# Embedding features: ScalarE multiplies x by the frequencies, VectorE takes off the rounding constant and subtracts the product in one operation

## The chip, the cores and the metric

The kernel runs on one core of one Trainium2 chip. A time is the device time of one execution in microseconds (us). The kernel before was timed three times: 1026.73, 1033.01 and 1031.65 us, so its median is 1031.65 us. The engines are TensorE (PE in the profile, its weight loads PEld), VectorE (DVE), ScalarE (ACT), GpSimd (POOL) and SyncE (SP, which only issues DMAs here).

## What is computed

A vision tower with one layer. The change lies in the first stage, the embedding of the tokens:

```
def _L0_tok_ref(xyz, freq_bands, W):          # xyz (4, 3, 512, 192), 6 frequencies 1, 2, 4 ... 32
    xb = 2.0 * jnp.pi * xyz[..., None] * freq_bands
    feat = jnp.concatenate([jnp.sin(xb), jnp.cos(xb)], axis=-1)
    feat = feat.reshape(b, n, -1)
    return jnp.einsum('bnf,of->bno', feat, W)  # 6912 features to 192
...
h = _L0_tok_ref(x, ...)
h = concatenate([cls_tok, h], axis=1)          # (4, 513, 192)
h = h + _L0_attn_ref(_layernorm(h), ...)       # attention with relative positions, 8 heads
h = h + _L0_ffn_ref(_layernorm(h), ...)        # attention over 12 heads, layer norms, 2 of 8 experts
```

The argument of the sine is first reduced to a part of one turn: with p = x*f, the kernel forms p minus the whole number nearest to p, and takes the sine of 2 pi times that. The cosine is the sine of pi/2 minus 2 pi times the absolute value of the same remainder. The nearest whole number comes from adding 12582912 (MAGIC) and taking it off again in float32.

## The kernel before

`embed_phase` works through four images. An image has 15 groups of features: groups 0 to 11 are "pairs" (two chunks of 128 input rows at one frequency, so a tile is 128 partitions x 1024), groups 12 to 14 are singles (128 x 512). A group passes through the engines like this:

- VectorE: `shift` (L202, near = x*f + MAGIC), `whole` (L207, near = near - MAGIC), `reduce` (L215, turn = x*f - near), `absolute` (L221, the absolute value of turn, put into near again).
- ScalarE: `group` takes the sine (L330, feat slot 0) and the cosine (L332, feat slot 1). For a pair, `first_parts` (L343) then rounds the features of the second chunk to a shorter format (parts 0), and VectorE's `rest` (L232) gives what is left (parts 1). In the first image each pair's weights are split the same way (L337 on ScalarE, L226 on VectorE).
- TensorE: 8 products with feat on plain float32 (16 MATMUL rows of L400), then for a pair 16 with the parts (L416 to L420). They add up in four PSUM banks over the whole image. When the last group is in, VectorE's `take_sums` copies the sums out (L238, L241) and takes statistics (L244, L249); TensorE may begin the next image's group 0 only when the first of the L241 additions is done.

Nothing plans the order: each engine has its program in written order, and semaphores join them. The tiles `feat`, `parts`, `near` and `turn` have three slots each (NF = 3), so group g uses slot g % 3. `feat_free` counts the groups that TensorE is done with; the sine of group g waits until group g - 3 is counted. `take_sums(b-1)` stands in VectorE's program at group 1 of image b, behind `rest` of group 0. `take_roots(b-1)` (two square roots on ScalarE, L348, which need another activation table) stands behind group 3, and `normalize(b-1)` (L253 to L261), which waits for it, at group 4 on VectorE. SP reloads x for the next image when `turn_done` says that the last group on a chunk has been reduced, and after the last x it fills a scratch area with zeros by 20 DMAs.

Of the kernel before, what the change touches and what calls it, by code (L numbers as in the profile page):

```python
# [8 lines left out]
ALU = mybir.AluOpType  # L9
ACT = mybir.ActivationFunctionType  # L10
# [7 lines left out]
B = 4  # L18
# [29 lines left out]
MAGIC = 12582912.0  # L48
NO_SIGN = 0x7FFFFFFF
TWO_PI = 6.283185307179586  # L50
EPS = 1e-5
BIG = 1e30
GROUPS = [(c0, 2, f) for c0 in (0, 2) for f in range(BANDS)] + [(4, 1, j) for j in range(BANDS // 2)]
UNITS = [(c0 + i, f) for c0, n, f in GROUPS for i in range(n)]
NE = len(GROUPS)
# [8 lines left out]
def stand_alone(eng, passed):  # L64


    eng.sem_inc(passed, 1)


def embed_phase(nc, s):  # L70

    NF = 3
    sem = s.sem
    x_in, w_in = [sem(f"x_in{c}") for c in range(5)], [sem(f"w_in{g}") for g in range(NE)]
    raw_in = [sem(f"raw_in{g}") for g in range(NE)]
    freq_in, ident_in, cls_in, zeroed = sem("freq_in"), sem("ident_in"), sem("cls_in"), sem("zeroed")
    consts_set, edges_set = sem("consts_set"), sem("edges_set")
    shifted, rounded, turn_done, aturn_done = sem("shifted"), sem("rounded"), sem("turn_done"), sem("aturn_done")
    sin_done, cos_done, feat_free, passed = sem("sin_done"), sem("cos_done"), sem("feat_free"), sem("turns_passed")
    w_hi, w_lo, hi_done, lo_done = sem("w_hi"), sem("w_lo"), sem("hi_done"), sem("feat_lo")  # L80
    pairs = [g for g in range(NE) if GROUPS[g][1] == 2]
# [9 lines left out]
    first_unit = [sum(n for _, n, _ in GROUPS[:g]) for g in range(NE)]  # L91
    with ExitStack() as ctx:
        sb = lambda n, sh, dt=F32: ctx.enter_context(nc.sbuf_tensor(n, sh, dt))
        x = sb("x", [128, 5, N])
        w = sb("w", [128, 2 * NE, D])
        raw = s.place.rearrange("p (g j n) -> p g j n", g=NPAIR, j=2)
        feat = sb("feat", [128, NF, 2, 2, N])
        w_parts = sb("w_parts", [128, NPAIR, 2, 2, D], F32R)
        parts = sb("parts", [128, NF, 2, 2, N], F32R)
        near = sb("near", [128, NF, 2, N])  # L100
        turn = sb("turn", [128, NF, 2, N])
        aturn = near
        tokens, h1_tok = sb("tokens", [128, 4, D]), sb("h1_tok", [128, 4, D])
        b2_rows, base = sb("b2_rows", [128, D]), sb("base", [128, 4, D])
        stats, mean_var = sb("stats", [128, 4, 6]), sb("mean_var", [128, 4, 2])
        roots, inv = sb("roots", [128, 2, 4]), sb("inv", [128, 2, 4])
        half_pi, eps = sb("half_pi", [128, 1]), sb("eps", [128, 2])
        freq = sb("freq", [128, NU])
# [78 lines left out]
        def _(dve):  # L187
# [4 lines left out]
            def shift(b, g, first):  # L192
                c0, n, f = GROUPS[g]
                u, r = first_unit[g], g % NF
                if f == 0:
                    for c in range(c0, c0 + n):
                        dve.wait_ge(x_in[c], b * 16 + 16)
                if g >= NF or not first:
                    dve.wait_ge(cos_done, b * NE + g - NF + 1)
                if not first:  # L200
                    stand_alone(dve, passed)
                dve.tensor_scalar(near[:, r, 0:n, :], x[:, c0:c0 + n, :], freq[:, u:u + 1], MAGIC, ALU.mult, ALU.add).then_inc(shifted, 1)  # L202

            def whole(b, g):
                n, r = GROUPS[g][1], g % NF
                dve.wait_ge(shifted, b * NE + g + 1)
                dve.tensor_scalar(near[:, r, 0:n, :], near[:, r, 0:n, :], MAGIC, None, ALU.subtract).then_inc(rounded, 1)  # L207

            def reduce(b, g, first):
                c0, n, f = GROUPS[g]  # L210
                u, r = first_unit[g], g % NF
                dve.wait_ge(rounded, b * NE + g + 1)
                if g >= NF or not first:
                    dve.wait_ge(sin_done, b * NE + g - NF + 1)
                dve.scalar_tensor_tensor(out=turn[:, r, 0:n, :], in0=x[:, c0:c0 + n, :], scalar=freq[:, u:u + 1], in1=near[:, r, 0:n, :],  # L215
                                         op0=ALU.mult, op1=ALU.subtract).then_inc(turn_done, 1)

            def absolute(b, g):
                n, r = GROUPS[g][1], g % NF
# [50 lines left out]
            def cls_norm():  # L270
                dve.wait_ge(cls_rooted, 1)
                dve.reciprocal(cls_inv[:, :], cls_roots[:, :]).then_inc(cls_rooted, 1)
                dve.wait_ge(cls_rooted, 2)
                for k, row in enumerate((s.y_cls[:, :], cls_row[:, 1, :])):
                    dve.tensor_scalar(row, cls_row[:, 0, :], cls_mean_var[:, 0:1], cls_inv[:, k:k + 1],
                                      ALU.subtract, ALU.mult).then_inc(cls_rows, 1)

            def image(b, first=False, more=True):
                for g in range(NE):
                    if first and g == 4:  # L280
                        cls_statistics()
                    if first and g == 8:
                        cls_norm()
                    if g + 1 < NE:
                        whole(b, g + 1)
                    elif more:
                        whole(b + 1, 0)
                    reduce(b, g, first)
                    if g + 2 < NE:
                        shift(b, g + 2, first)  # L290
                    elif more:
                        shift(b + 1, g + 2 - NE, False)
                    absolute(b, g)
                    if g - 1 in pairs:
                        rest(b, g - 1)
                    if first and g in pairs:
                        split_weights(g)
                    if not first and g == 1:
                        take_sums(b - 1)
                    if not first and g == 4:  # L300
                        normalize(b - 1)

            dve.wait_ge(freq_in, 16)
            shift(0, 0, True)
            shift(0, 1, True)
            whole(0, 0)
            image(0, first=True)
            dve.wait_ge(cls_flipped, 1)
            dve.tensor_copy(cls_col[:, :], cls_flip[0:DC, 0:2]).then_inc(cls_cols_set, 1)
# [5 lines left out]
            with dve.Fori(1, B - 1) as b:  # L315
                image(b)
# [5 lines left out]

        @block.scalar
        def _(act):
            def group(b, g, first):
                n, r = GROUPS[g][1], g % NF
                act.wait_ge(turn_done, b * NE + g + 1)
                if g >= NF or not first:
                    act.wait_ge(feat_free, b * NE + g - NF + 1)
                act.activation(feat[:, r, 0, 0:n, :], turn[:, r, 0:n, :], ACT.Sin, scale=TWO_PI).then_inc(sin_done, 1)  # L330
                act.wait_ge(aturn_done, b * NE + g + 1)
                act.activation(feat[:, r, 1, 0:n, :], aturn[:, r, 0:n, :], ACT.Sin,  # L332
                               bias=half_pi[:, :], scale=-TWO_PI).then_inc(cos_done, 1)

            def split_weights(g):
                act.wait_ge(raw_in[g], 16)
                act.copy(w_parts[:, g, :, 0, :], raw[:, g]).then_inc(w_hi, 1)  # L337

            def first_parts(b, g):
                r = g % NF  # L340
                act.wait_ge(sin_done, b * NE + g + 1)
                act.wait_ge(cos_done, b * NE + g + 1)
                act.copy(parts[:, r, 0], feat[:, r, :, 1, :]).then_inc(hi_done, 1)  # L343

            def take_roots(i):
                act.wait_ge(aggregated, i * 4 + 4)
                for k in range(2):
                    root = act.activation(roots[:, k, :], mean_var[:, :, 1], ACT.Sqrt, bias=eps[:, k:k + 1],  # L348
                                          scale=1.0 + EPS * k)
                root.then_inc(rooted, 1)  # L350

            def take_h1(i):
                for c in range(2):
                    act.wait_ge(h1_flipped, i * 2 + 2 + c + 1)
                    act.activation(s.h1T[0:DC, c, bass.ds(i, 1), 1:L].rearrange("p b n -> p (b n)"), flip[c][0:DC, :], ACT.Copy,
                                   scale=norm1[:, c:c + 1]).then_inc(h1_out, 1)

            act.wait_ge(consts_set, 3)
            act.sem_inc(rooted, 1)
            act.sem_inc(h1_out, 2)  # L360
            for g in range(NE):
                if g == 6:
                    act.wait_ge(cls_stated, 2)
                    for k in range(2):
                        root = act.activation(cls_roots[:, k:k + 1], cls_mean_var[:, 1:2], ACT.Sqrt, bias=eps[0:1, k:k + 1], scale=1.0 + EPS * k)
                    root.then_inc(cls_rooted, 1)
                group(0, g, True)
                if g in pairs:
                    split_weights(g)
                    first_parts(0, g)  # L370
            with act.Fori(1, B) as b:
                for g in range(NE):
                    group(b, g, False)
                    if g in pairs:
                        first_parts(b, g)
                    if g == 3:
                        take_roots(b - 1)
                    if g == 10:
                        take_h1(b - 1)
            take_roots(B - 1)  # L380
            take_h1(B - 1)

# [1964 lines left out]
```

## Time and profile before

| what | value |
|---|---|
| median of three runs | 1031.65 us |
| profiled execution, its own time | 1030.35 us |
| its span (what the profile covers) | 1028.6 us |
| granted TensorE clock, mean over the span | 0.949 of full speed |
| PE busy over the span | 911.2 us (89%) |
| PEld busy over the span | 798.0 us (78%) |
| DVE busy over the span | 721.2 us (70%) |
| ACT busy over the span | 653.4 us (64%) |
| the embedding, first DMA to last feature product | about 0 to 294 us |

The shares are averages over stages that differ. What the change does must be read in the first 300 us. A granted clock of 1.00 is 2.4 GHz and 0.50 is 1.2 GHz. In the first microseconds of the program the view says 1.00 although the matmuls there take about twice as long as later.

### The profile page before, as it was taken

The numbers are of one execution on the slowest core, as the hardware profiler recorded it, in microseconds if no ns is written. First come the engines' busy times: TensorE is split into PE (matmuls) and PEld (weight loads), VectorE is DVE, ScalarE is ACT, GpSimd is POOL, SyncE is SP. The second block draws the span as 40 slices with busy tenths as digits, with TensorE's granted clock in tenths as the row PEclk, the third lists the DMA queues.
The fourth block names the chain that finished last, engine by engine and source line by source line (L and its number), as shares of the span: only waits on it lengthen the run. The fifth ranks groups of instructions, "written<-read, shape, count | busy, mean of one in ns | idle before, by whom it ended". The sixth has DMA issues, their size and how long they took to land. (4 is left out here: it accounts for less than half of the span.)

```text
span 1028.6 us, 20033 instructions
## 1 busy us (share of the span) xinstructions
PE 911.2 (89%) x6459; PEld 798.0 (78%) x6459; DVE 721.2 (70%) x1690; ACT 653.4 (64%) x1223; POOL 141.9 (14%) x204
## 2 busy tenths in 40 slices
PE   5999999999987898889887988799699995799995
PEld 5899999999975777567666766677498874799993
DVE  7899979979833885478637864697566245688764
ACT  5766757848625886588748864797553332686661
POOL 1000000000000244114411431054300000000000
PEclk9999999999988999999999999999799997799995
DMA  8003100089703684269416951596300120533101
GB/s 264 22 21 96 37 31 25 31 129 154 119 17 109 191 278 128 66 188 295 136 52 184 290 157 35 166 299 186 104 1 1 32 77 16 163 108 108 55 1 62
DMA packets 83798, 114.06 MB, mean 111 GB/s; under 512 B 12271, under 2 KB 44476, under 8 KB 83724
## 3 DMA queue, kind: packets, MB, share of 16 engines
q1 hardware_dynamic: 83724, 113.18, 39.8%
q8 instruction: 34, 0.56, 0.2%
q14 instruction: 40, 0.33, 0.1%
HBM read 62.31 MB, written 47.67 MB: 107 GB/s over the span
## 5 line engine op out<-in xcount | busy, mean ns | idle before, releaser
L400 PE MATMUL psum<-w,feat 128*128 128x192 f32 x960 | 168.2, 330 | 13.7 <-ACT feat L330 10.2
L400 PEld LDWEIGHTS psum<-w,feat 128*128 128x128 f32 x960 | 156.9, 192 | 14.6 <-issue 10.1
L615 POOL TENSOR_SCALAR a_scores<-a_scores,a_inv 112x514 f32<-112x514 f32 (+1 forms) x160 | 112.9, 707 | 290.8 <-DVE a_inv L964 290.3
L949 DVE CUSTOM_DVE_ANT_0 a_scores<-psum,a_bias 112x514 f32<-112x514 f32 (+1 forms) x160 | 109.8, 688 | 49.2 <-PE psum L688 42.1
L837 ACT ACTIVATE a_scores<-a_scores,a_least 112x514 f32<-112x514 f32 (+1 forms) x160 | 116.6, 729 | 13.7 <-DVE a_least L949 13.1
L418 PE MATMUL psum<-w_parts,parts 128*128 128x384 f32 x368 | 113.5, 373 | 3.3 <-DVE parts L232 2.8
L701 PE MATMUL psum<-ident,a_scores 112*112 112x112 f32 (+1 forms) x800 | 102.3, 260 | 14.1 <-DVE a_probsT L959 8.2
L330 ACT ACTIVATE feat<-turn 128x1024 f32<-128x1024 f32 (+1 forms) x60 | 58.4, 974 | 85.7 <-DVE turn L215 53.9
L688 PE MATMUL psum<-a_kh,a_q 128*112 128x258 f32 (+1 forms) x320 | 101.2, 337 | 7.1 <-DVE a_q L919 4.2
L701 PEld LDWEIGHTS psum<-ident,a_scores 112*112 112x112 f32 (+1 forms) x800 | 77.5, 136 | 35.6 <-POOL a_scores L615 18.4
L642 PE MATMUL psum<-h1T,place 96*128 (+3 forms) x320 | 86.9, 410 | 13.3 <-DVEq L912 6.9
L420 PE MATMUL psum<-w_parts,parts 128*128 128x192 f32 x384 | 96.6, 252 | 0.0
L832 ACT COPY a_probsT<-psum 112x336 f32<-112x336 f32 (+1 forms) x160 | 66.6, 416 | 39.2 <-PE psum L701 35.2
L688 PE MATMUL psum<-a_kl,a_q 128*112 128x258 f32 (+1 forms) x320 | 85.6, 287 | 0.0
L671 PE MATMUL psum<-a_table,a_qpos 96*112 96x257 bf16 (+1 forms) x320 | 66.3, 289 | 16.2 <-ACT a_pos L824 14.2
L824 ACT COPY a_pos<-psum 112x514 f32<-112x514 f32 (+1 forms) x100 | 58.9, 589 | 33.4 <-PE psum L671 27.0
L642 PEld LDWEIGHTS psum<-h1T,place 96*128 96x128 f32 (+1 forms) x320 | 60.6, 204 | 24.0 <-DVEq L912 8.2
L418 PEld LDWEIGHTS psum<-w_parts,parts 128*128 128x128 f32 x368 | 69.2, 188 | 5.4 <-issue 5.3
L420 PEld LDWEIGHTS psum<-w_parts,parts 128*128 128x128 f32 x384 | 73.3, 191 | 0.0
L959 DVE COPY a_probsT<-psum 112x224 f32<-112x224 f32 (+1 forms) x160 | 58.8, 367 | 17.2 <-PE psum L701 16.8
L688 PEld LDWEIGHTS psum<-a_kh,a_q 128*112 128x112 f32 (+1 forms) x320 | 55.3, 173 | 19.8 <-issue 12.7
L215 DVE SCALAR_TENSOR_TENSOR turn<-x,freq,near 128x1024 f32<-128x1024 f32 (+1 forms) x60 | 70.2, 1170 | 0.0
(285 smaller groups left out, 1822.6 us busy)
## 6 DMA issues: line engine op xcount, KB each, us to landing
shear<-a_pos SPq DMA_DIRECT2D x128, 224.9 KB, 3.7
a_bias<-shear SPq DMA_DIRECT2D x128, 224.4 KB, 3.8
shear<-zero SPq DMA_DIRECT2D x20, 448.9 KB, 16.4
e_fc<-in_e_fc_dram SPq DMA_DIRECT2D x16, 384.0 KB, 3.9
x<-in_xT_dram SPq DMA_DIRECT2D x20, 256.0 KB, 3.0
e_proj<-in_e_proj_dram SPq DMA_DIRECT2D x8, 576.0 KB, 5.3
shear<-a_pos SPq DMA_DIRECT2D x32, 130.5 KB
a_bias<-shear SPq DMA_DIRECT2D x32, 130.3 KB
```

The lines of the kernel that those rows point to most:

```text
L215: dve.scalar_tensor_tensor(out=turn[:, r, 0:n, :], in0=x[:, c0:c0 + n, :], scalar=freq[:, u:u + 1], in1=near[:, r, 0:n, :], op0=ALU.mult, ...
L400: mm = pe.matmul(sums[m][:, 0:D], feat[:, r, j, 0, 128 * m:128 * m + 128], w[:, k, :], start=begins, stop=ends)
L418: pe.matmul(sums[m][:, 0:2 * D], f(0), w_parts[:, g, j, :, :].rearrange("p a n -> p (a n)"), start=False, stop=False)
L420: mm = pe.matmul(sums[m][:, 0:D], f(1), w_parts[:, g, j, 0, :], start=False, stop=False)
L615: pool.tensor_scalar(row, row, inv[0:TILES[g % NT][1], g % TT:g % TT + 1], 1.0, ALU.mult, ALU.mult).then_inc(weighed, 1)
L642: mm = pe.matmul(out[:, 0:HALF], wt[0:rows, c, 128 * p:128 * p + 128], x, start=c == 0, stop=c == 1)
L671: mm = pe.matmul(pairs[2][w][0:r, 0:HALF], qpos[:, h, i0:i0 + r], table[:, w * HALF:w * HALF + HALF], start=True, stop=True)
L688: mm = pe.matmul(pairs[score_pair(g)][w][0:r, 0:HALF + 1], q[:, h, i0:i0 + r], k[:, h, w * HALF:w * HALF + HALF + 1], start=k is kh, stop= ...
L701: mm = pe.transpose(pairs[3][jb // 3][0:TILE, TILE * (jb % 3):TILE * (jb % 3) + r], scores[0:r, g % TT, TILE * jb:TILE * jb + TILE], s.ide ...
L832: act.copy(probsT[:, slot(g // NT), 0:3, i0:i0 + r], src).then_inc(put_a, 1)
L837: act.activation(scores[0:r, g % TT, 0:PADL], scores[0:r, g % TT, 0:PADL], ACT.Exp, bias=least[0:r, g % TT:g % TT + 1], scale=-1.0, accum_ ...
L949: dve.tensor_tensor_reduce(halves(scores[0:r, g % TT, 0:PADL]), psum2(score_pair(g), r), halves(bias[0:r, g % MR, :]), -1.0 / 8, BIG, ALU. ...
```

## The change

VectorE's `whole` goes. ScalarE gets a new step, `scale_x`: it writes x*f into `scaled_x`, which is no tile of its own but slot r of `feat[:, :, 0]`, the place where the sine of the same group is written later. VectorE's `reduce` now reads near and `scaled_x` and gives (near - MAGIC) - x*f, the remainder with its sign turned, so the scale of the sine becomes -2 pi. On ScalarE the order is `scale_x` of group g + 1, then sine and cosine of group g (`waves`), and what followed. The wait for `feat_free` moves from the sine of group g to `scale_x` of group g, with the same count (group g - 3 done). VectorE's program is turned too: `reduce` of g, then `shift` of g + 1, where it had been `whole` of g + 1, `reduce` of g, `shift` of g + 2. The wait of `reduce` for an old sine goes, and one for `scaled` comes.

```
+        scaled_x = feat[:, :, 0]
...
-            def whole(b, g):
-                n, r = GROUPS[g][1], g % NF
-                dve.wait_ge(shifted, b * NE + g + 1)
-                dve.tensor_scalar(near[:, r, 0:n, :], near[:, r, 0:n, :], MAGIC, None, ALU.subtract).then_inc(rounded, 1)
-
-            def reduce(b, g, first):
-                c0, n, f = GROUPS[g]
-                u, r = first_unit[g], g % NF
-                dve.wait_ge(rounded, b * NE + g + 1)
-                if g >= NF or not first:
-                    dve.wait_ge(sin_done, b * NE + g - NF + 1)
-                dve.scalar_tensor_tensor(out=turn[:, r, 0:n, :], in0=x[:, c0:c0 + n, :], scalar=freq[:, u:u + 1], in1=near[:, r, 0:n, :],
-                                         op0=ALU.mult, op1=ALU.subtract).then_inc(turn_done, 1)
+            def reduce(b, g):
+                n, r = GROUPS[g][1], g % NF
+                dve.wait_ge(shifted, b * NE + g + 1)
+                dve.wait_ge(scaled, b * NE + g + 1)
+                dve.scalar_tensor_tensor(out=turn[:, r, 0:n, :], in0=near[:, r, 0:n, :], scalar=MAGIC, in1=scaled_x[:, r, 0:n, :],
+                                         op0=ALU.subtract, op1=ALU.subtract).then_inc(turn_done, 1)
...
+                    reduce(b, g)
                     if g + 1 < NE:
-                        whole(b, g + 1)
+                        shift(b, g + 1, first)
...
         @block.scalar
-            def group(b, g, first):
+            def scale_x(b, g, first):
+                c0, n, f = GROUPS[g]
+                u, r = first_unit[g], g % NF
+                if f == 0:
+                    for c in range(c0, c0 + n):
+                        act.wait_ge(x_in[c], b * 16 + 16)
+                if g >= NF or not first:
+                    act.wait_ge(feat_free, b * NE + g - NF + 1)
+                act.activation(scaled_x[:, r, 0:n, :], x[:, c0:c0 + n, :], ACT.Copy, scale=freq[:, u:u + 1]).then_inc(scaled, 1)
+
+            def waves(b, g):
                 n, r = GROUPS[g][1], g % NF
                 act.wait_ge(turn_done, b * NE + g + 1)
-                if g >= NF or not first:
-                    act.wait_ge(feat_free, b * NE + g - NF + 1)
-                act.activation(feat[:, r, 0, 0:n, :], turn[:, r, 0:n, :], ACT.Sin, scale=TWO_PI).then_inc(sin_done, 1)
+                act.activation(feat[:, r, 0, 0:n, :], turn[:, r, 0:n, :], ACT.Sin, scale=-TWO_PI).then_inc(sin_done, 1)
...
+            def image(b, more):
                 for g in range(NE):
-                    group(b, g, False)
+                    if g + 1 < NE:
+                        scale_x(b, g + 1, False)
+                    elif more:
+                        scale_x(b + 1, 0, False)
+                    waves(b, g)
                     if g in pairs:
                         first_parts(b, g)
                     if g == 3:
                         take_roots(b - 1)
```

How the change moves instructions is seen in the order of an engine's program; a bracket names the semaphores that a row waits for. On ScalarE, where images 0 and 1 meet: before, from the sine of the last group (128x512) to the features of group 0 of the next image (L330 sine, L332 cosine, L343 parts).

```order
L330 ACTIVATE feat<-turn 128x512 [waits feat_free,turn_done]
L332 ACTIVATE feat<-near,half_pi 128x512 [waits aturn_done]
L371 UNCONDITIONAL_BRANCH
L371 ISA
L329 REGISTER_ALU [waits turn_done]
L330 ACTIVATE feat<-turn 128x1024 [waits feat_free]
L332 ACTIVATE feat<-near,half_pi 128x1024 [waits aturn_done]
L343 CAST parts<-feat 128x1024 [waits cos_done,sin_done]
```

The same place with the change (L321 is `scale_x`, of group 0 in the first row and of group 1 in the sixth; L326 the sine, L328 the cosine, L338 the parts):

```order
L321 ACTIVATE feat<-x,freq 128x1024 [waits feat_free,x_in1,x_in0]
L326 ACTIVATE feat<-turn 128x512 [waits turn_done]
L328 ACTIVATE feat<-near,half_pi 128x512 [waits aturn_done]
L387 UNCONDITIONAL_BRANCH
L387 ISA
L321 ACTIVATE feat<-x,freq 128x1024 [waits feat_free]
L325 REGISTER_ALU
L326 ACTIVATE feat<-turn 128x1024 [waits turn_done]
L328 ACTIVATE feat<-near,half_pi 128x1024 [waits aturn_done]
L338 CAST parts<-feat 128x1024 [waits cos_done,sin_done]
```

The sine of group 0 stood behind a wait for TensorE's group 12 of the image before; now it stands behind `scale_x` of group 1, which waits for group 13.

On ScalarE, at the square roots behind group 3 of an image: before, from the roots to the parts of group 4.

```order
L348 ACT_TABLE_LOAD
L348 ACTIVATE roots<-mean_var,eps 128x4 [waits aggregated]
L348 ACTIVATE roots<-mean_var,eps 128x4
L327 REGISTER_ALU
L330 ACT_TABLE_LOAD [waits feat_free]
L330 ACTIVATE feat<-turn 128x1024 [waits turn_done]
L332 ACTIVATE feat<-near,half_pi 128x1024 [waits aturn_done]
L343 CAST parts<-feat 128x1024 [waits cos_done,sin_done]
```

With the change, from the parts of group 3 to the sine of group 4:

```order
L338 CAST parts<-feat 128x1024 [waits cos_done,sin_done]
L341 ISA
L343 ACT_TABLE_LOAD
L343 ACTIVATE roots<-mean_var,eps 128x4 [waits aggregated]
L343 ACTIVATE roots<-mean_var,eps 128x4
L321 ACTIVATE feat<-x,freq 128x1024 [waits feat_free]
L325 REGISTER_ALU
L326 ACT_TABLE_LOAD
L326 ACTIVATE feat<-turn 128x1024 [waits turn_done]
```

The roots and both table loads now have `scale_x` of group 5 among them, and that waits for TensorE's group 2 where the sine of group 4 had waited for group 1.

At the program's start ScalarE now has one table load more, and its first one waits for x (L321 `scale_x` of groups 0 and 1, L326 the sine of group 0):

```order
L321 ACT_TABLE_LOAD [waits consts_set,freq_in,x_in1]
L321 ACTIVATE feat<-x,freq 128x1024 [waits x_in0]
L321 ACTIVATE feat<-x,freq 128x1024
L326 ACT_TABLE_LOAD
L326 ACTIVATE feat<-turn 128x1024 [waits turn_done]
```

Before, one load stood there that waited for constants only; the sine followed it.

## Rows read from the trace of the kernel before

**Rows 1.** Windows: busy time of each engine in image 0 and image 1
```profile
core 0: us, PE busy (x) PEld busy (x) DVE busy (x) ACT busy (x) POOL busy (x), PEclk, DMA share, GB/s
24.31:78.59 54.28, 51.03 (x324) 48.87 (x323) 48.54 (x71) 37.60 (x44) 0.00 (x0) 1.00 0.06 21
88.24:156.18 67.94, 67.94 (x444) 67.64 (x444) 61.54 (x94) 45.34 (x47) 1.81 (x1) 1.00 0.08 26
```

**Rows 2.** Waits in 0 to 300 us: total, times, longest
```profile
PE psum L400 <- DVE tokens L241: 3.6, 3, 1.7
```

**Rows 3.** Lines by form: count, busy us, mean ns, idle before and its releasers
```profile
L215 DVE SCALAR_TENSOR_TENSOR turn<-x,freq,near 128x1024 f32<-128x1024 f32 x48 | 61.3, 1277 | 0.0
L232 DVE TENSOR_TENSOR parts<-feat,parts 128x1024 fp32r<-128x1024 f32 x48 | 58.4, 1217 | 0.6 <-ACT parts L343 0.6
L332 ACT ACTIVATE feat<-near,half_pi 128x1024 f32<-128x1024 f32 x48 | 55.0, 1146 | 6.3 <-DVE near L221 6.2
L330 ACT ACTIVATE feat<-turn 128x1024 f32<-128x1024 f32 x48 | 50.9, 1060 | 55.4 <-DVE turn L215 51.8 <-PE psum L400 2.6 <-PE psum L420 0.8
L343 ACT CAST parts<-feat 128x1024 fp32r<-128x1024 f32 x48 | 50.4, 1049 | 3.1
L202 DVE TENSOR_SCALAR near<-x,freq 128x1024 f32<-128x1024 f32 x48 | 35.8, 747 | 15.3 <-ACT feat L332 11.1 <-DMA x<-in_xT_dram 4.2
L207 DVE TENSOR_SCALAR near<-near 128x1024 f32<-128x1024 f32 x48 | 33.6, 702 | 0.2 <-DVE h1T L312 0.2
L221 DVE TENSOR_SCALAR near<-turn 128x1024 uint32<-128x1024 uint32 x48 | 32.8, 684 | 0.0
```

**Rows 4.** Timeline, DVE, where image 0 ends: start us, us, engine, line, op
```profile
85.65 1.22 DVE L232 TENSOR_TENSOR parts<-feat,parts 128x1024 fp32r<-128x1024 f32 x1
86.78 1.14 DVE L238 COPY tokens<-psum 128x192 f32<-128x192 f32 x4
87.85 1.14 DVE L241 TENSOR_TENSOR tokens<-tokens,psum 128x192 f32<-128x192 f32 x4
```

**Rows 5.** Timeline, PE, groups 0, 1 and 2 of image 1
```profile
88.24 2.87 PE L400 MATMUL psum<-w,feat 128*128 128x192 f32 x16 [1.67 <-DVE tokens L241]
93.42 2.78 PE L400 MATMUL psum<-w,feat 128*128 128x192 f32 x16
98.34 2.78 PE L400 MATMUL psum<-w,feat 128*128 128x192 f32 x16
```

**Rows 6.** Timeline, ACT, groups 2 to 4 of image 1 with the roots between
```profile
93.98 1.15 ACT L332 ACTIVATE feat<-near,half_pi 128x1024 f32<-128x1024 f32 x1 [0.20 <-DVE near L221]
95.22 1.05 ACT L343 CAST parts<-feat 128x1024 fp32r<-128x1024 f32 x1
...
100.48 1.28 ACT L348 ACT_TABLE_LOAD   x1
...
102.27 1.28 ACT L330 ACT_TABLE_LOAD   x1
103.57 1.06 ACT L330 ACTIVATE feat<-turn 128x1024 f32<-128x1024 f32 x1
104.53 1.14 ACT L332 ACTIVATE feat<-near,half_pi 128x1024 f32<-128x1024 f32 x1
```

**Rows 7.** Timeline, DVE, `normalize` at group 4 of image 1, first instruction and the one behind
```profile
103.39 0.19 DVE L253 RECIPROCAL inv<-roots 128x8 f32<-128x8 f32 x1
...
106.16 0.69 DVE L207 TENSOR_SCALAR near<-near 128x1024 f32<-128x1024 f32 x1
```

**Rows 8.** Timeline, the start: x arrives for DVE, first products on PE
```profile
5.10 1.42 DVE L202 TENSOR_SCALAR near<-x,freq 128x1024 f32<-128x1024 f32 x2 [4.16 <-DMA x<-in_xT_dram]
...
10.15 5.09 PE L400 MATMUL psum<-w,feat 128*128 128x192 f32 x16 [10.15 <-ACT feat L330]
```

**Rows 9.** Windows, PE alone, three stretches of a later stage: busy, PEclk, DMA
```profile
516.80:518.40 1.60, 0.00 (x0) 1.00 0.25 62
...
519.90:523.30 3.40, 3.40 (x17) 0.50 0.22 56
...
734.90:748.50 13.60, 8.69 (x37) 0.50 0.70 196
```

More of the change, by code:

```diff
@@ L77, in embed_phase @@
     consts_set, edges_set = sem("consts_set"), sem("edges_set")
-    shifted, rounded, turn_done, aturn_done = sem("shifted"), sem("rounded"), sem("turn_done"), sem("aturn_done")
+    scaled, shifted, turn_done, aturn_done = sem("scaled"), sem("shifted"), sem("turn_done"), sem("aturn_done")
     sin_done, cos_done, feat_free, passed = sem("sin_done"), sem("cos_done"), sem("feat_free"), sem("turns_passed")
@@ L283, in image @@
                         cls_norm()
+                    reduce(b, g)
                     if g + 1 < NE:
-                        whole(b, g + 1)
+                        shift(b, g + 1, first)
                     elif more:
[L287 to L292, printed above, removed]
+                        shift(b + 1, 0, False)
                     absolute(b, g)
@@ L304, in _ @@
             shift(0, 0, True)
-            shift(0, 1, True)
-            whole(0, 0)
             image(0, first=True)
@@ L324, in _ @@
         def _(act):
-            def group(b, g, first):
+            def scale_x(b, g, first):
[8 more added lines that the diff above has]
+            def waves(b, g):
                 n, r = GROUPS[g][1], g % NF
                 act.wait_ge(turn_done, b * NE + g + 1)
-                if g >= NF or not first:
-                    act.wait_ge(feat_free, b * NE + g - NF + 1)
-                act.activation(feat[:, r, 0, 0:n, :], turn[:, r, 0:n, :], ACT.Sin, scale=TWO_PI).then_inc(sin_done, 1)
+                act.activation(feat[:, r, 0, 0:n, :], turn[:, r, 0:n, :], ACT.Sin, scale=-TWO_PI).then_inc(sin_done, 1)
                 act.wait_ge(aturn_done, b * NE + g + 1)
-                act.activation(feat[:, r, 1, 0:n, :], aturn[:, r, 0:n, :], ACT.Sin,
-                               bias=half_pi[:, :], scale=-TWO_PI).then_inc(cos_done, 1)
+                act.activation(feat[:, r, 1, 0:n, :], aturn[:, r, 0:n, :], ACT.Sin, bias=half_pi[:, :], scale=-TWO_PI).then_inc(cos_done, 1)
             def split_weights(g):
@@ L358, in _ @@
             act.wait_ge(consts_set, 3)
+            act.wait_ge(freq_in, 16)
             act.sem_inc(rooted, 1)
             act.sem_inc(h1_out, 2)
+            scale_x(0, 0, True)
             for g in range(NE):
@@ L366, in _ @@
                     root.then_inc(cls_rooted, 1)
-                group(0, g, True)
+                if g + 1 < NE:
+                    scale_x(0, g + 1, True)
+                else:
+                    scale_x(1, 0, False)
+                waves(0, g)
                 if g in pairs:
@@ L370, in _ @@
                     first_parts(0, g)
-            with act.Fori(1, B) as b:
+            def image(b, more):
                 for g in range(NE):
-                    group(b, g, False)
+                    if g + 1 < NE:
+                        scale_x(b, g + 1, False)
+                    elif more:
+                        scale_x(b + 1, 0, False)
+                    waves(b, g)
                     if g in pairs:
@@ L379, in _ @@
                         take_h1(b - 1)
+            with act.Fori(1, B - 1) as b:
+                image(b, True)
+            image(B - 1, False)
             take_roots(B - 1)
```

## The prediction

> **What bounds the kernel now.** I read the windows first, to find which engine is full where the change acts. In image 1 TensorE is busy for all 67.94 us of its products and VectorE for 61.54, ScalarE for 45.34 [rows 1]. In image 0, which also splits the weights, TensorE is busy 51.03 of 54.28 us [rows 1]. The waits say where TensorE stands still between images: three times, 3.6 us together, the longest 1.7, each time for the first token addition [rows 2]; the longest is the 1.67 us between images 0 and 1 [rows 5], so the other two are about 0.95. The lines say that ScalarE's 55.4 us of idling ahead of the sine is mostly for VectorE's reduction [rows 3]. ScalarE idles because VectorE is slow, but that is not what ends the stage: TensorE is. All that a quicker VectorE can return is TensorE's idle time, 54.28 - 51.03 = 3.25 us in image 0 and 3.6 us at the three boundaries.
>
> **What is removed.** L207, 48 pairs of 0.70 us = 33.6 us of VectorE [rows 3], and 12 singles. It lies beside TensorE's work in images 1 to 3, so it is worth nothing there. L215 keeps its kind: one fused operation on two float32 tiles, 1.28 us [rows 3]. That its scalar is now a constant I cost at nothing.
>
> **What is added.** ScalarE's product. No row has it. The sine without a column operand takes 1.06 us, the cosine with one 1.15 and the cast 1.05 [rows 3]; the product reads a column of frequencies, so I take the cosine's 1.15 (bounds 1.05 and 1.15). The next activation starts about 0.1 before the end of one (103.57 to 104.53 for 1.06 us) [rows 6]. A pair then costs ScalarE about 1.05 + 0.96 + 1.24 + 1.05 = 4.3 us, where 1.24 is from cosine to cast [rows 6], against TensorE's 98.34 - 93.42 = 4.92 [rows 5]. In the steady run ScalarE keeps up, with 0.6 us to spare.
>
> **What is moved is the real cost.** The product of group g + 1 lies in the slot of its sine, so it waits for TensorE's group g - 2, and the sine of group g is queued behind it. Before, the sine of g waited for g - 3 only. ScalarE, and what hangs on it, loses one group of lead, and the product on top. Steady: if TensorE is done with group g - 2 at T, the product starts at T + 0.1, the sine at 1.15, the cosine at 2.1, the cast at 3.35, its end at 4.4, VectorE's rest (1.22 us [rows 3]) ends at 5.65. TensorE needs it 4.92 + 2.65 = 7.6 after T. It is covered, with 2 us left. So every interruption of ScalarE or VectorE that is longer than 2 us now shows on TensorE. There are two per image.
>
> **The boundary.** Count from TensorE's last product of an image. Sixteen products of a single take about 2.7 us [rows 5], so group 13 is done at -2.7. ScalarE: product of group 1 at -2.6, sine of group 0 at -1.55, cosine at -0.6, cast at 0.65, ended at 1.7. VectorE's own steps for groups 0 and 1 (1.28 + 0.75 + 0.68 [rows 3] from the product of group 1 at -1.45) are over at 1.0, so the rest of group 0 starts at 1.75. `take_sums` stands behind it: copies 1.13 us later (85.65 to 86.78 [rows 4]), at 2.9, and TensorE starts 1.46 after the first copy (86.78 [rows 4] to 88.24 [rows 5]), at 4.35. That replaces 3.6 us over three boundaries by 3 x 4.35 = 13.05: **+9.45 us**.
>
> **The roots.** Count from TensorE's start on group 0; group 1 starts at 5.18 and each pair takes 4.92 [rows 5], so groups 2, 3 and 4 at 10.1, 15.0 and 19.95. ScalarE: product of 4 at 10.2, sine, cosine and cast of group 3, cast ended at 14.5; first table load and roots 102.27 - 100.48 = 1.79 [rows 6], to 16.3; product of 5 to 17.45, second load 1.28 to 18.75, sine of 4 ended at 19.8, in time; cosine at 19.7, cast ended at 22.0. VectorE: `normalize` from 16.35, 2.77 us long (103.39 to 106.16 [rows 7]), to 19.1, then three steps to 21.6, then rest of group 4 from 22.05 to 23.25. TensorE wants it at 19.95 + 2.65 = 22.6. A stall of 0.65 us, in three images: **+1.95 us**. The take-over of the transposed tokens behind group 10 is shorter than the 2 us of cover: nothing.
>
> **Image 0.** The gain is at most its 3.25 us of idling. Against it: the first table load now waits for x, which comes at 5.10 [rows 8], and a second follows, so the first sine is ready at about 5.1 + 1.3 + 2.2 + 1.3 + 1.05 = 10.95, where TensorE began at 10.15; and the two loads with the roots of the class token (about 1.8 + 1.3 = 3.1 us) interrupt ScalarE when it has 0.1 to 0.6 us to spare. Both together are about 3 us. I take **0** (bounds -3.3 and +3). The row shows a load of 1.28 us, and the sine behind it starts 0.02 later (102.27 + 1.28, 103.57) [rows 6]. The Trainium skill, page "ScalarE: Activation LUTs", section "What ACT_TABLE_LOAD costs", counts 1.38 us of drain on top for every switch. By that the added switch at the start would make the sum 1.4 us more, which lies inside the forecast's own range; the row shows no drain, and I go by the row.
>
> **The clock.** Until now TensorE never stands still for more than 1.67 us inside the embedding, and the clock there is 1.00 [rows 1, 5]. With 4.35 us it will not stay so: in a later stage an idle stretch of 1.60 us was enough, once, to be followed by 3.40 us of full work at 0.50 [rows 9]. That costs 1.7 us of products. The program's start, after a longer rest, cost 5.09 - 2.78 = 2.3 us on sixteen products [rows 5, 8]. The worst stretch at half clock in rows 9 lasted 13.60 us, 6.8 us if it fell on full work. I take the nearest row, 1.7 us at each of three boundaries: **+5.1 us** (bounds 0 and 20).
>
> **The DMAs.** The filling with zeros starts when the last x is in, and so some us later than before, and has the whole of image 3 to run in: nothing.
>
> **Sum.** 9.45 + 1.95 + 0 + 5.1 = 16.5 us. The profiled execution took 1030.35 us (span 1028.6), so 1046.9; it stands 1.3 us below the median of 1031.65. I predict 1047 us.
>
> **Rivals.**
> 1. *The stalls come, the clock holds, wholly or nearly.* For it: rows 1 show 1.00 over all of the images, and 1.67 us of rest did not move it. Against it: rows 9. 1030.35 + 11.4 = 1041.8 to 1043. Chance 0.22.
> 2. *The half clock lasts longer, or ScalarE's spare 0.6 us is not there.* If semaphore and issue times take it, ScalarE becomes the bound: 0.2 us more per pair over 36 pairs is 7 us; or the clock costs 3.5 us a boundary. 1052 to 1062. Chance 0.13.
> 3. *The relief wins; not slower.* Place: VectorE's path to `take_sums`. If the rest of group 0 were over before TensorE's last product, the copies would start as soon as the sums are there, TensorE would wait 0.95 us at all three boundaries (0.7 less than now in sum), and image 0 would run at TensorE's pace, up to 3.25 us less: 1030.35 - 4 = 1026.4, and with part of it 1026 to 1036. It decides at the point where ScalarE starts group 0's sine 2.9 us earlier than I have it, which needs the product of group 1 to be issued about 3 us sooner. For it speaks that VectorE gets 33.6 us back and that ScalarE has 22 us idle in image 1. Against it stands the written wait for group 13. Chance 0.15.
> 4. *The change does not do what it says*, for instance the product costs far less or the operations fall apart otherwise: 0.02, anywhere.
>
> **Chances and range.** The forecast itself, 1043 to 1052, has 0.48. Within 1% (about what a measurement of this kernel can tell from no change; 1021.3 to 1042.0) lies nearly all of rival 3 and somewhat more than half of rival 1: 0.28. Faster by over 1% would need more than all of TensorE's idle time in the stage: 0.03. Slower by over 1%: 0.69. The range takes in the forecast, rival 1, the lower part of rival 2 and the upper end of rival 3: 1035 to 1056.
>
> **What would show it.** The waits of L400's successor for the token addition should be about 4.4 us at each of the three boundaries, up from 3.6 in all. ScalarE's idle time ahead of its product should be put down to TensorE, and that ahead of the sine should nearly vanish. VectorE should idle some 25% of images 1 to 3. TensorE should wait 0.6 us for the rest of group 4. The granted clock should show 0.50 for some 3.4 us at each boundary. The product should take 1.05 to 1.15 us. I am wrong if TensorE's waits at the boundaries stay below 2 us, or if it waits in the middle of images for every group.

## The result, and the profile after

| | median us | runs | profiled execution, span |
|---|---|---|---|
| before | 1030.06 | 4 | 1030.35, 1028.6 |
| with the change | 1047.37 (1042.80 to 1050.67) | 4 | 1050.67, 1048.8 |

The ratio is 1.0151, 95% interval 1.0104 to 1.0198. That is 16 us slower by the ratio and 17 us by the medians, 1047.37 us where 1047 was forecast. On a second chip it was 1.018 (1.0136 to 1.0225). The ratios in this document are taken over fast executions alone and are not exactly the quotients of the medians (1.0168 here). The two spans differ by more than the medians, 20.2 us.

The engines moved as the change says. The profile of the changed kernel (busy time and share of the span of each engine, and its instructions) shows VectorE lighter by 31 us and ScalarE heavier by 54 us, and the time went up all the same.

```profile
PE 918.0 (88%) x6459; PEld 803.4 (77%) x6459; DVE 689.8 (66%) x1630; ACT 707.5 (67%) x1284; POOL 142.0 (14%) x204
```

The waits of the changed kernel in the first 320 us (who waited for whom: total us, times, longest) answer to [rows 2] in their second line.

```profile
ACT feat L321 <- PE psum L430: 54.2, 34, 6.8
...
PE psum L410 <- DVE tokens L235: 13.0, 3, 4.3
...
PE psum L428 <- DVE parts L226: 5.6, 8, 2.5
```

TensorE now waits 13.0 us for the token additions, 3.6 before. ScalarE waits 54.2 us ahead of its new product (L321), for TensorE; the 51.8 us ahead of the sine [rows 3] are gone. The idle time changed its owner: it was put down to VectorE and is now put down to TensorE. Most of it costs nothing, because ScalarE waits there for an engine that is full. It costs where TensorE itself runs dry, and that is what the rows on the boundaries show.

The boundary of images 0 and 1 on ScalarE, in order of time (start, length, engine, line; the bracket is the idle time before):

```profile
85.23 1.16 ACT L321 ACTIVATE feat<-x,freq 128x1024 f32<-128x1024 f32 x1 [0.24 <-PE psum L410]
86.30 1.04 ACT L326 ACTIVATE feat<-turn 128x1024 f32<-128x1024 f32 x1
87.24 1.13 ACT L328 ACTIVATE feat<-near,half_pi 128x1024 f32<-128x1024 f32 x1
88.46 1.04 ACT L338 CAST parts<-feat 128x1024 fp32r<-128x1024 f32 x1
```

and on VectorE, which answers to [rows 4]:

```profile
89.53 1.23 DVE L226 TENSOR_TENSOR parts<-feat,parts 128x1024 fp32r<-128x1024 f32 x1 [0.55 <-ACT parts L338]
90.68 1.15 DVE L232 COPY tokens<-psum 128x192 f32<-128x192 f32 x4
```

and on TensorE, the first products of images 1, 2 and 3, and group 1 of image 1, which answer to [rows 5]:

```profile
92.14 5.49 PE L410 MATMUL psum<-w,feat 128*128 128x192 f32 x16 [4.34 <-DVE tokens L235]
100.25 2.78 PE L410 MATMUL psum<-w,feat 128*128 128x192 f32 x16
...
168.23 5.31 PE L410 MATMUL psum<-w,feat 128*128 128x192 f32 x16 [4.34 <-DVE tokens L235]
...
243.71 5.12 PE L410 MATMUL psum<-w,feat 128*128 128x192 f32 x16 [4.34 <-DVE tokens L235]
```

The last sum is over at 92.14 - 4.34 = 87.80. Counted from there the product of group 1 starts at -2.57, the sine at -1.5, the cosine at -0.56, the cast at 0.66, the rest at 1.73, the copies at 2.88, TensorE at 4.34. And the sixteen products behind the wait take 5.1 to 5.5 us, not 2.87: windows of TensorE over the same boundary (stretch, length, busy, granted clock, DMA share, GB/s) show why. A pass is one MATMUL row of the trace; the number of them is in brackets.

```profile
84.00:88.00 4.00, 3.80 (x24) 1.00 1.02 288
88.00:92.00 4.00, 0.00 (x0) 0.91 0.83 221
92.00:96.00 4.00, 3.86 (x12) 0.50 0.02 4
96.00:100.00 4.00, 4.00 (x25) 0.73 0.00 0
100.00:104.00 4.00, 4.00 (x28) 1.00 0.00 0
```

The granted clock falls before the work comes back, is at its lower level (1.2 GHz) in the stretch in which it comes back, and 12 passes start in these 4 us where 28 do at the upper one (last row).

Group 4 of image 1, the other predicted stall:

```profile
118.44 0.41 PE L428 MATMUL psum<-w_parts,parts 128*128 128x384 f32 x1 [0.65 <-DVE parts L226]
```

Group 4 as a whole took from 115.01 to 120.81 us, 5.80 us, where it had taken 4.92. In images 2 and 3 it took 5.77 and 5.84 (4.92 and 4.88 before). So the stall cost 0.9 us an image, 2.7 us in all, a little more than the wait that the row shows.

**Where the stage ends.** The later stages are unchanged, and take a different time in each run, so the end of the embedding tells the kernels apart better than the whole. I read it at the first product behind the last token sums (L474, L464 before), which starts at 316.19 us and started at 295.30: **+20.9 us**. Behind that point 732.6 us were left, 733.3 before. The repeat of the changed kernel has 314.69 and 741.3: the stage is the same within 1.5 us, and the rest of the kernel 9 us longer with no instruction changed.

### The profile page after: what moved, and what is told of

Its sections match the earlier page's. It is cut to its first block and busy times, and to the rows that moved or that the text cites. A ratio compares the mean times of both kernels' runs of the same rounds, so it can differ in the third digit from the quotient of the medians.

```text
span 1048.8 us, 19976 instructions
## 1 busy us (share of the span) xinstructions
PE 918.0 (88%) x6459; PEld 803.4 (77%) x6459; DVE 689.8 (66%) x1630; ACT 707.5 (67%) x1284; POOL 142.0 (14%) x204
## 5 line engine op out<-in xcount | busy, mean ns | idle before, releaser
L410 PE MATMUL psum<-w,feat 128*128 128x192 f32 x960 | 176.0, 341 | 23.8 <-DVE tokens L235 13.0
L410 PEld LDWEIGHTS psum<-w,feat 128*128 128x128 f32 x960 | 164.1, 199 | 24.7 <-DVE tokens L235 13.9
L321 ACT ACTIVATE feat<-x,freq 128x1024 f32<-128x1024 f32 (+1 forms) x60 | 63.6, 1061 | 57.5 <-PE psum L430 54.2
L209 DVE SCALAR_TENSOR_TENSOR turn<-near,feat 128x1024 f32<-128x1024 f32 (+1 forms) x60 | 67.8, 1130 | 42.4 <-ACT feat L321 42.1
L226 DVE TENSOR_TENSOR parts<-feat,parts 128x1024 fp32r<-128x1024 f32 x48 | 58.7, 1222 | 21.9 <-ACT parts L338 21.9
```

Of the source, the lines that this page charges most:

```text
L209: dve.scalar_tensor_tensor(out=turn[:, r, 0:n, :], in0=near[:, r, 0:n, :], scalar=MAGIC, in1=scaled_x[:, r, 0:n, :], op0=ALU.subtract, op1 ...
L410: mm = pe.matmul(sums[m][:, 0:D], feat[:, r, j, 0, 128 * m:128 * m + 128], w[:, k, :], start=begins, stop=ends)
```

## The experiments

The rows were measured on three chips. A row is compared with the kernel before on the same chip, whose median is 1033.16 us, or the one in brackets. The stage's end is from one profiled run each; two such runs of the same changed kernel differ by 1.5 us.

| kernel | median us | ratio to before (95%) | TensorE's waits for the token additions | stage ends |
|---|---|---|---|---|
| before | 1033.16 | | 1.67, 0.95, 0.95 | 295.30 |
| the change, again | 1051.18 | 1.0180 (1.0136 to 1.0225) | 4.34, 4.34, 4.34 | 314.69 |
| product in the slot of turn | 1024.33 | 0.9932 (0.9897 to 0.9966) | 2.3 in sum | 290.39 |
| products in the gap | 1043.53 | 1.0087 (1.0049 to 1.0124) | (filled) | 307.32 |
| sums first | 1043.31 | 1.0118 (1.0061 to 1.0174) | 2.57, 2.56, 2.56 | 308.11 |
| before, tight wait | 1045.48 (before: 1030.81) | 1.0140 (1.0090 to 1.0189) | 4.16, 3.55, 3.55 | 304.69 |
| slot of turn, early table load | 1023.98 (1030.81) | 0.9913 (0.9871 to 0.9955) | 2.3 in sum | 288.56 |
| slot of turn, again | 1026.92 (1030.81) | 0.9964 (0.9931 to 0.9997) | 2.2 in sum | 290.71 |
| slot of turn, early table load, again | 1023.09 (1032.52) | 0.9869 (0.9823 to 0.9916) | 2.2 in sum | 288.53 |
| the same, TensorE busy at the start | 1022.20 (1032.52) | 0.9892 (0.9851 to 0.9932) | 2.2 in sum | 288.09 |

**The change, again.**

> The changed kernel once more, beside the kernels below on one chip. Both theories: 1.012 to 1.020 of the kernel before, with 4.34 us of TensorE waiting at each of the three boundaries.

Measured 1.018, with waits of 4.34 us three times, as expected.

**Is it the slot, or ScalarE's load?** The product goes to another slot; everything else stays.

```
-        scaled_x = feat[:, :, 0]
+        scaled_x = turn
...   scale_x
                 if g >= NF or not first:
-                    act.wait_ge(feat_free, b * NE + g - NF + 1)
+                    act.wait_ge(sin_done, b * NE + g - NF + 1)
...   waves
+                if g >= NF or not first:
+                    act.wait_ge(feat_free, b * NE + g - NF + 1)
```

> The product x*f goes into the slot of turn, where the reduction then works in place, and no longer into the slot of the sine; the wait for feat_free goes back to the sine. ScalarE does the same instructions in the same order. Theory of the slot (the product waits for TensorE's group g-2 and costs the lead): TensorE waits 0.95 us at each boundary, 0 at group 4, the clock stays at 1.00 in images 1 to 3, image 0 runs at most 3 us quicker than before; 1024 to 1031 us, 0.995 to 1.001 of the kernel before. Rival, the load of ScalarE (4.3 us more busy per pair and a table load among them): the waits stay above 3 us and the time at 1040 or more.

Measured 0.9932, and 0.9964 on another chip: the first a little better than the 0.995 to 1.001 that was expected, the second within it. The slot of turn is free for the product as soon as the sine and the absolute value of group g - 3 are done, both long over, and the reduction reads and writes it in place. ScalarE has the same 54.8 us of pair products, with no idle time before them, and TensorE waits 0.7 to 0.8 us at the boundaries. The line by form, and TensorE's waits over the first 330 us:

```profile
L321 ACT ACTIVATE turn<-x,freq 128x1024 f32<-128x1024 f32 x48 | 54.8, 1143 | 0.0
```

```profile
PE psum L412 <- DVE tokens L235: 2.3, 3, 0.8
```

TensorE at the first boundary (0.71 us of waiting, where it was 4.34):

```profile
83.68 2.87 PE L412 MATMUL psum<-w,feat 128*128 128x192 f32 x16 [0.71 <-DVE tokens L235]
```

The same boundary in windows of TensorE, with nothing at half clock:

```profile
80.00:84.00 4.00, 3.29 (x21) 1.00 0.35 81
84.00:88.00 4.00, 4.00 (x31) 1.00 0.02 4
```

The rival, ScalarE's load, falls: ScalarE's load and order are unchanged and the stage ends 24 to 26 us sooner than with the change. What the change costs, it costs through the place of its product and the wait that this place brings. And with that place mended the idea gains, 4.6 to 4.9 us at the stage's end.

**What does the half clock cost?** Ten products that nobody needs go into TensorE's gap at each boundary.

```
                         if begins and not first:
+                            if m == 0:
+                                for _ in range(10):
+                                    pe.matmul(s.bank[7][:, 0:D], s.ident[:, :], w[:, 0, :], start=True, stop=True)
                             pe.wait_ge(tokens_done, b * 4 - 3 + m)
```

> The changed kernel with ten more products of 128x192 at the head of TensorE's wait at each boundary, into a PSUM bank that nobody reads; they compute nothing that is needed. About 3.5 us of work in a gap of 4.34 us. Theory (of the 8 us or so that the three boundaries cost beyond their waiting, the half clock is the cause): the token additions still come 4.3 us after the last sum, the clock stays at 1.00, group 0 takes 5.2 us and not 8.1, and the time falls by 8 us to about 1039 (1.008 of before). Rival (group 0 is slow because its inputs are late, or the products disturb the wait): 1047 or more.

TensorE at the first boundary, the added work in the first row:

```profile
87.12 3.51 PE L411 MATMUL psum<-w,ident 128*128 128x192 f32 x20 [0.40 <-PE psum L413]
91.06 2.87 PE L413 MATMUL psum<-w,feat 128*128 128x192 f32 x16 [0.43 <-DVE tokens L235]
96.22 1.00 PE L413 MATMUL psum<-w,feat 128*128 128x192 f32 x5
```

```profile
88.00:92.00 4.00, 3.57 (x23) 1.00 0.65 156
92.00:96.00 4.00, 4.00 (x31) 1.00 0.01 4
```

The sums end at 86.72 and the products of image 1 still start 4.34 us later, but group 0 takes 96.22 - 91.06 = 5.16 us, not 8.11, and the clock stays at 1.00. The median falls by 7.6 us against the change beside it (1051.18 to 1043.53), the stage's end by 7.4, from 314.69 to 307.32. Doing useless work in a gap makes the kernel quicker. The rival (late inputs, or products that disturb the wait) falls, and the clock term is shown: about 2.5 us a boundary.

**Is the boundary the chain that was walked?** The chain loses one of its links: `take_sums` comes ahead of the rest of group 0.

```
+                    if not first and g == 1:
+                        take_sums(b - 1)
                     if g - 1 in pairs:
                         rest(b, g - 1)
                     if first and g in pairs:
                         split_weights(g)
-                    if not first and g == 1:
-                        take_sums(b - 1)
```

> The changed kernel with VectorE's take_sums ahead of the rest of group 0 and not behind it. Theory (the boundary is the chain product of group 1, sine, cosine, cast, rest, sums): the sums no longer wait for the cast, TensorE's wait falls from 4.34 to about 2.45 us (VectorE is free at 0.95, and 1.46 more), 1.9 us less at three boundaries; the clock still falls, for less. 1039 to 1043 us, 1.009 to 1.013. Rival (TensorE's wait comes from the sums themselves or from the clock): the wait stays at 4.3 us and the time at 1047; or what is won is lost again, since the rest of group 0 is 3.7 us later and the products of group 0 wait for it.

Measured 2.57, 2.56 and 2.56 us where 2.45 was worked out; 1.0118, inside what was expected. The copies start as soon as VectorE is through with `absolute` of group 1 and no longer wait for a cast. The clock fell behind the first two of these waits and not behind the third. The later rest of group 0, which the expectation named as a possible loss, shows at the third boundary, where TensorE waits 1.00 us for it. Image 1 and image 3 on TensorE:

```profile
90.80 4.55 PE L410 MATMUL psum<-w,feat 128*128 128x192 f32 x16 [2.57 <-DVE tokens L235]
...
236.52 2.87 PE L410 MATMUL psum<-w,feat 128*128 128x192 f32 x16 [2.56 <-DVE tokens L235]
...
240.38 0.44 PE L426 MATMUL psum<-w_parts,parts 128*128 128x192 f32 x2 [1.00 <-DVE parts L226]
```

The windows at the first boundary and at the third:

```profile
92.00:96.00 4.00, 4.00 (x19) 0.60 0.01 5
96.00:100.00 4.00, 4.00 (x29) 1.00 0.01 4
236.00:240.00 4.00, 2.87 (x16) 1.00 1.24 154
```

**How much is the lead alone?** The kernel before with the count of one wait raised by one, so that the sine gets the wait that the changed kernel's order forces on it.

```
-                if g >= NF or not first:
-                    act.wait_ge(feat_free, b * NE + g - NF + 1)
+                if g >= NF - 1 or not first:
+                    act.wait_ge(feat_free, b * NE + g - NF + 2)
```

> The kernel before, unchanged but for one number: the sine of group g waits until TensorE is done with group g-2 and not g-3. No product on ScalarE, all of VectorE's steps as before. It prices the lost lead by itself. By the walk of the boundary without the product: sine of group 0 at -2.6 us from TensorE's last sum, cast at -0.4, rest from 0.7 to 1.85, TensorE starts at 3.3. So the theory expects waits of about 3.3 us at three boundaries (9.9 in sum, 3.6 before), a half clock behind most of them, and 1037 to 1045 us (1.006 to 1.014 of before). Rival (the lead alone is harmless, the product in front of the sine is what costs): waits below 2 us and a time within 0.3% of before.

TensorE's waits are 4.16, 3.55 and 3.55 us, 11.3 in sum (3.3 each was worked out; at the first boundary VectorE's own late steps add 0.6). So where the change adds 9.45 us of waiting at the boundaries, this kernel adds 7.7 without any product. The rival (the lost lead is harmless) falls. The time is 1.014, at the upper edge of what was expected, and the trace does not give all of it to the stage: its end moved by 9.4 us, the median by 14.7. Behind the stage 739.6 us were left (733.3 before), where no instruction differs. A half clock had been expected behind most of the waits; it fell behind the one of 4.16 us and not behind those of 3.55:

```profile
90.00:94.00 4.00, 3.32 (x12) 0.57 0.02 4
...
163.00:167.00 4.00, 3.42 (x23) 1.00 0.00 0
...
235.00:239.00 4.00, 3.83 (x27) 1.00 1.12 143
```

**The table loads at the start.** Built on the better kernel:

```
             act.wait_ge(consts_set, 3)
+            act.activation(s.idle[:, :], half_pi[:, :], ACT.Sin)
             act.wait_ge(freq_in, 16)
```

> The kernel with the product in the slot of turn, and a sine of one column into an unused tile as ScalarE's first activation, so that the sine's table is loaded while x is still on its way and the product of group 0 finds a table. Theory: TensorE's first product comes at about 8.8 us and not at 11.0, two table loads (2.6 us) go off the path; 2 us less than the same kernel without it, 0.991 to 0.993 of before. Rival (the first features are late for x or the weights): the first product stays at 10 us or later.

ScalarE's start in this kernel:

```profile
0.74 1.28 ACT L356 ACT_TABLE_LOAD   x1 [0.74 <-PEq L2351]
2.03 0.20 ACT L356 ACTIVATE idle<-half_pi 128x1 f32<-128x1 f32 x1
5.16 2.19 ACT L321 ACTIVATE turn<-x,freq 128x1024 f32<-128x1024 f32 x2 [2.92 <-DMA x<-in_xT_dram]
7.68 1.06 ACT L328 ACTIVATE feat<-turn 128x1024 f32<-128x1024 f32 x1 [0.33 <-DVE turn L209]
```

With the change the first of these had been a load that waited for x (4.79 us), and the sine came at 9.58; with the product in the slot of turn it came at 9.75. TensorE's first product now comes at 8.88, expected 8.8; the stage ends 1.8 to 2.2 us sooner than without. In time, 0.9913 here and 0.9869 in a repeat; on one chip with the kernel without it the intervals overlap, so the 2 us are shown by the trace and not by the times.

> The kernel with the product in the slot of turn again, beside the one above on the same chip: 0.990 to 0.997 of before.

Measured 0.9964, just inside.

> The kernel with the product in the slot of turn and the early table load again, beside the one below: 0.989 to 0.996 of before, first product of features at 8.9 us.

Measured 0.9869, a little better than expected, with the first product at 8.85.

**A warm start.** On top of that, TensorE gets products of zeros before the features come. The question is whether its slow beginning can be avoided:

```
             pe.sem_inc(h1_flipped, 2)
+            pe.wait_ge(edges_set, 1)
+            for _ in range(11):
+                pe.matmul(s.bank[7][:, 0:171], zero[:, 0:128], zero[:, 0:171], start=True, stop=True)
```

> The same, with eleven products of zeros by zeros at TensorE's start, from about 1 us to 7 or 8 us, into a bank that nobody reads; their results are not used. Theory (TensorE's clock at a start or behind a wait depends on what it did just before): the first sixteen products of features take about 2.8 us of work and not 4.7, the rest of group 0 is then the bound at the start, so at most 1 us is won, which shows in the trace and not in the time. Rival (the first products are slow for their inputs or the DMAs): still 4.7 us.

```profile
1.03 5.65 PE L401 MATMUL psum<-zero 112*128 112x171 f32 x22 [1.03 <-POOL zero L174]
8.88 4.52 PE L416 MATMUL psum<-w,feat 128*128 128x192 f32 x16 [2.20 <-ACT feat L328]
```

The expectation missed: 4.52 us against 4.77 without, where 2.8 was expected. The added work was over at 6.68, 2.2 us before the features came. This does not make the rival (slow inputs) right: in this run the view gives a granted clock of 0.53 from 8.8 to 11.0 us, so the first products were slow with the lower clock. Whether a longer run of it, or one of other numbers, would hold the clock was not tried. 0.9892 is no different from 0.9869.

## Why the prediction was right, step by step

**What bounds the stage**: right. TensorE, not VectorE. Taking 31 us off VectorE could return only what TensorE had been idle. The kernel with the product in the slot of turn has the relief and none of the stalls, and returns 4.9 us at the stage's end. The prediction's 3.25 us for image 0 was read too low: the window of rows 1 covers 54.3 of the image's 76.4 us. From its first product to its last sum the image took 72.0 us in that kernel, 4.4 less; the boundaries gave 1.3 and the later start took 0.8. In the changed kernel the image took 77.0 us, so the bound did not enter the result. Rival 3 was this kernel, and its condition (the product of group 1 issued sooner) is what the experiment supplied; in the change as made it does not hold.

**The product's price**: 1.15 us taken, 1146 ns measured.

```profile
L321 ACT ACTIVATE feat<-x,freq 128x1024 f32<-128x1024 f32 x48 | 54.9, 1146 | 41.8 <-PE psum L430 38.5 <-PE psum L410 3.3
L209 DVE SCALAR_TENSOR_TENSOR turn<-near,feat 128x1024 f32<-128x1024 f32 x48 | 59.5, 1239 | 26.1 <-ACT feat L321 25.8
```

**The boundary**: 4.35 us walked, 4.34 measured, at all three. +9.45 us, as in the sum. Taking out the last link moved it to where the walk puts it.

**The roots**: 0.65 us walked, 0.6, 0.6 and 0.7 measured in images 1 to 3: +1.9 us. The stall is gone in the kernel whose sine has its lead back. It was not undone by itself. The group as a whole lost 2.7 us in three images, which is 0.7 more than the waits.

**Image 0**: 0 taken. TensorE began at 10.78 (10.95 walked, 10.15 before), and the last sum of image 0 ended at 87.80 in the first run and 91.02 - 4.34 = 86.68 in the repeat, 86.57 before: +1.2 and +0.1. TensorE waited 2.47 us at group 6, behind the two table loads for the class token on ScalarE (a wait of 1.40 before); the first run had 3.4 us of half clock behind that, the repeat had none. Inside the bounds.

**The clock**: the one term that was too small. 1.7 us a boundary was taken from a stretch of 3.4 us at half clock; group 0 took 8.11, 7.62 and 7.42 us where it had taken 5.16 to 5.19, so 2.9, 2.4 and 2.3, in sum 7.6 and not 5.1. The better row had been in hand: the start, sixteen products in 5.09 instead of 2.78 us [rows 5, 8], 2.3 us. A loss of 2.3 to 2.9 us at half pace means 4.5 to 5.9 us of work at 1.2 GHz (an estimate from these differences), where the forecast had 3.4. The stretch in rows 9 was of another kind: between the rest of 1.60 us and the half clock lie 1.5 us of work (518.40 to 519.90), so it began in the middle of work and not behind the rest.

The other signs: ScalarE's idle time ahead of the sine is 0.1 us, and VectorE idles 29, 28 and 33% of images 1 to 3, where some 25% was said.

The terms as measured, 1.2 + 9.45 + 2.7 + 7.6 = 20.95, make up the stage's 20.9 us. The forecast for the profiled execution was 1046.9; it took 1050.67. That the median met 1047 nearly to the digit is partly luck: the unchanged stages alone vary by 9 us between profiled runs.

**The added drain**, 1.4 us by the Trainium skill, page "ScalarE: Activation LUTs", section "What ACT_TABLE_LOAD costs": the trace does not agree. The sine starts at 9.58 where the second load ends at 8.29 + 1.28 = 9.57, and that load starts where the second product ends, at 6.08 + 2.19 = 8.27.

```profile
4.79 1.28 ACT L321 ACT_TABLE_LOAD   x1 [4.79 <-DMA x<-in_xT_dram]
6.08 2.19 ACT L321 ACTIVATE feat<-x,freq 128x1024 f32<-128x1024 f32 x2
8.29 1.28 ACT L326 ACT_TABLE_LOAD   x1
9.58 1.06 ACT L326 ACTIVATE feat<-turn 128x1024 f32<-128x1024 f32 x1
```

## What to carry to other kernels

Before handing work from a busy engine to an idle one, ask where its result will lie: a borrowed slot brings the slot's wait with it, and that wait moved ahead of the sine and took a group of lead from everything queued behind it. Ask also which engine is full; relief for an engine beside the full one returns at most the full one's idle time. Cover is spent at the interruptions (image ends, square roots), so walk those and not the steady run, and where the clock fell behind a wait, count the slow work as part of the wait.

## What the hardware showed that I had not expected

The granted clock does not follow from the length of a wait alone. At the image boundaries it fell behind waits of 4.34 us 6 times of 6; behind 4.16 us once of once; behind two of 3.55 us not at all; behind three of about 2.56 us twice; behind 1.67 us and less never. At group 6 of image 0 a wait of 2.44 to 2.48 us was followed by the lower clock in two runs of four. And behind the last sums of the stage, where TensorE waits 1.59 or 1.60 us in every run, the next 32 small products took 2.90 or 2.93 us in four runs and 3.49 to 4.97 in seven. The same kernel gave both:

```profile
290.39 2.90 PE L476 MATMUL psum<-x 64*97 64x32 f32 x32 [1.59 <-DVE tokens L235]
```

```profile
290.71 4.45 PE L476 MATMUL psum<-x 64*97 64x32 f32 x32 [1.59 <-DVE tokens L235]
```

In the second of these runs the granted clock reads 0.50 from 292 us on, in the middle of the products; what decides is open. Filling three gaps with 3.5 us of useless products each saved 7.6 us in all.

VectorE's fused operation with a constant in the place of the column of frequencies takes 1239 ns, 1277 before [rows 3]. I had put nothing down for it; it did not matter here.
